# A graph network on one core: the GINE pass takes its neighbour sums from the count matrix, and the attention pass sums the edge attributes

## What is computed

```python
# attention: softmax over the edges of a target (and a self loop), 4 heads
alpha = exp(leaky_relu(a_src[src] + a_dst[dst]) - amax[dst]); alpha /= segment_sum(alpha, dst)[dst]
x = layernorm(x + segment_sum(h[src] * alpha, dst).reshape(N, 256) @ Wl + ...)
# deviation of the neighbours
x = layernorm(x + std of x[src] per dst)
# GINE, with 64 attributes per edge
agg = segment_sum(x[src] + (edge_attr @ We_w + We_b), dst)
x = layernorm(x + relu(((1 + eps) * x + agg) @ W1 + b1) @ W2 + b2)
# four SAGE convolutions 64 -> 128 -> 32 -> 128 -> 64
agg = segment_sum(h[src], dst) / max(deg, 1);  h = agg @ Wl.T + bl + h @ Wr.T
x = layernorm(x + h4)
```

## Time and profile before

| | |
|---|---|
| median of 3 runs | 11377.18 us (11374.62 to 11385.63) |
| span of the profiled execution | 11372.6 us |
| busy, share of the span | PE 65%, POOL 50%, DVE 45%, ACT 16% |
| chain that ended last | PE 35%, issue 19%, DVE 15%, POOL 14%, DVE's queue 11%, DMA 5% |
| DMA | 1416 MB, 125 GB/s mean, 540705 of 977746 packets under 512 bytes |

### The profile page before, as it was taken

How to read it: one execution, slowest core, us unless ns; L and a number is a source line. 1 busy time by engine, 2 the same in 40 slices (tenths; PEclk the granted TensorE clock), 3 DMA queues, 4 the chain that set the end, 5 groups by cost and what they waited for, 6 DMA issues and landing times.

```text
span 11372.6 us, 263999 instructions
## 1 busy us (share of the span) xinstructions
PE 7339.2 (65%) x67389; PEld 5512.0 (48%) x67390; DVE 5137.7 (45%) x13935; ACT 1762.8 (16%) x3566; POOL 5690.5 (50%) x5555
## 2 busy tenths in 40 slices
PE   5888877775466666777954444455677455555676
PEld 4766766664122111445533334445666444444666
DVE  4555555555887777444332233333332333322343
ACT  2333333332033454000000000000000000000000
POOL 4777766553000000753037777776553765653654
PEclk7888888887788899788975555666777676667777
DMA  2333322222012233555532222224556576555566
GB/s 60 74 72 75 73 69 66 65 58 58 18 72 90 113 136 148 160 157 170 179 105 51 54 56 56 57 59 126 187 198 213 183 257 235 183 195 211 201 235 208
DMA packets 977746, 1416.36 MB, mean 125 GB/s; under 512 B 540705, under 2 KB 649761, under 8 KB 970914
## 3 DMA queue, kind: packets, MB, share of 16 engines
q1 hardware_dynamic: 689858, 1130.79, 29.0%
q0 software_dynamic: 184832, 224.29, 9.0%
q10 hardware_dynamic: 102752, 58.62, 1.7%
HBM read 1197.73 MB, written 215.36 MB: 124 GB/s over the span
## 4 chain that ended last, share of the span: by engine, by line
PE 35%; issue 19%; DVE 15%; POOL 14%; DVEq 11%; DMA 5%; ACT 1%; SPq 0%; POOLq 0%; ACTq 0%
PE ps_turn L965 15%; POOL ARENA L650 14%; PE ps_out L811 5%; PE ps_turn L921 4%; DMA ARENA<-counts 3%; PE ps_turn L784 2%; PE ps_pair L811 2%; DVE onehots L1760 2%; DVEq L1774 2%; DVE ARENA L1683 2%; DVE ARENA L1681 1%; PE ps_turn L722 1%; PE ps_pair L846 1%; PE ps_pair L993 1%; DVEq L1688 1%
## 5 line engine op out<-in xcount | busy, mean ns | idle before, releaser
L650 POOL DMA_INDIRECT ARENA<-table_sage,idx x1920 | 1911.9, 996 | 1578.9 <-DVE idx L1755 1041.3
L965 PE MATMUL ps_turn<-ARENA 128*128 128x96 bf16 (+2 forms) x24010 | 2273.8, 260 | 474.5 <-DMA ARENA<-counts 193.2
L965 PEld LDWEIGHTS ps_turn<-ARENA 128*128 128x128 bf16 x24010 | 1847.1, 105 | 896.2 <-issue 589.9
L650 POOL DMA_INDIRECT ARENA<-table_gat,idx x1568 | 1733.1, 1105 | 857.0 <-issue 454.8
L650 POOL DMA_INDIRECT ARENA<-table_gine,idx x1568 | 1541.5, 983 | 964.9 <-issue 953.0
L921 PE MATMUL ps_turn<-ARENA 128*128 128x392 bf16 (+1 forms) x4204 | 1067.6, 360 | 668.0 <-DVE ARENA L1683 458.3
L650 POOL DMA_INDIRECT ARENA<-table_dev,idx x480 | 485.2, 1011 | 1735.5 <-DVE idx L1755 1599.5
L993 PE MATMUL ps_pair<-ARENA,onehots 128*128 128x32 bf16 (+2 forms) x10140 | 685.4, 224 | 931.2 <-DVE ARENA L1767 799.8
L1681 DVE TENSOR_SCALAR ARENA<-ARENA 128x784 bf16<-128x784 f16 (+1 forms) x2102 | 1007.1, 479 | 361.0 <-issue 229.0
L811 PE MATMUL ps_out<-ARENA,onehots 128*128 128x256 f32 (+1 forms) x3136 | 843.8, 432 | 505.5 <-DMA ARENA<-table_gine,idx 351.3
L993 PEld LDWEIGHTS ps_pair<-ARENA,onehots 128*128 x10140 | 562.3, 115 | 1059.7 <-issue 1058.4
(11 more groups left out here) (297 smaller groups left out, 7394.1 us busy)
## 6 DMA issues: line engine op xcount, KB each, us to landing
ARENA<-counts SPq DMA_DIRECT2D x1470, 448.0 KB
counts<-ARENA SPq DMA_DIRECT2D x49, 3136.0 KB, 9.0
ARENA<-counts SPq DMA_DIRECT2D x490, 224.0 KB
ARENA<-dst_b SPq DMA_DIRECT2D x393, 256.0 KB
ARENA<-edge_attr SPq DMA_DIRECT2D x390, 128.0 KB, 2.5
ARENA<-table_sage,idx POOLq DMA_INDIRECT x1920
ARENA<-table_gat,idx POOLq DMA_INDIRECT x1568
ARENA<-table_gine,idx POOLq DMA_INDIRECT x1568
```

Source lines behind the costliest of these rows:

```text
L650: pool.indirect_dma_start(ps["buf"][:, s, c, 0:ps["row"]], None, ps["table"][:, :], bass.IndirectOffsetOnAxis(idx[:, s, c:c + 1], 0)).then ...
L965: last = pe.matmul(ps_dense[half][:, 0:n], RING[:, b, :], XP[:, b, :], start=(b == PIECE_AT[pieces[0]]), stop=(j == pieces[-1] and b == PI ...
```

## The change

The gine pass becomes a dense pass with 64 columns in three parts (`parts=3, row=3 * D`). So dev's node step now stores its rows in three bf16 parts, as the passes before the SAGE passes do. The edge attributes are summed in gat: they are loaded into 64 further columns of the message buffer, the message matmul is 320 columns wide, and `GATW` becomes 325. The sums go to DRAM after each block (`edge_sums`) and come back as `ESUM` for gine's node step. The wider accumulator takes the place of `X` in gat: each block's old rows are loaded from the input again (`old_x`), new rows stand in the accumulator until the pass is over, and three copies then move them to `X`. SRAM areas move accordingly (`WHOLE`, `gat_area`). Edge attributes are padded on the host.

```diff
-GATW = H * D + H + 1
+MSGW = H * D + D
+GATW = MSGW + H + 1
...
-            dict(name="gine", parts=1, n=2 * D, row=D),
+            dict(name="gine", parts=3, n=D, row=3 * D),
...
-        STORING = ["gat", "gine", "sage1", "sage2", "sage3"]
+        STORING = ["gat", "dev", "gine", "sage1", "sage2", "sage3"]
...
-        X = sb("X", [P, TILES, D])
-        ARENA = sb("ARENA", [P, 33602])
+        WHOLE = sb("ARENA", [P, TILES * D + 33602])
+        X = WHOLE[:, 33602:33602 + TILES * D].rearrange("p (t d) -> p t d", d=D)
+        ARENA = WHOLE[:, 0:33602]
...
+        ACC_AT = TILES * D + 33602 - TILES * GATW
+        ACC = WHOLE[:, ACC_AT:ACC_AT + TILES * GATW]
...
-                if passes[k - 1]["parts"] == 1:
-                    with sp.Fori(0, BLOCKS) as b:
-                        load_nodes(b, b)
+                if passes[k - 1]["name"] == "dev":
+                    with sp.Fori(0, STEPS) as b:
+                        load_nodes(b, b + STEPS)
+                    with sp.Fori(0, STEPS) as b:
+                        load_nodes(b + STEPS, b)
+                    sp.wait_ge(rows_ready[k], BLOCKS)
+                    sp.dma_start(ESUM.rearrange("p t d -> p (t d)"), edge_sums).then_inc(edge_sums_loaded, 16)
...
-                            last = pe.matmul(sums[:, 0:H * D if gat else n], lhs, rhs, start=(c == 0 and q == 0), stop=(c == C - 1 and q == parts - 1))
+                            last = pe.matmul(sums[:, 0:MSGW if gat else n], lhs, rhs, start=(c == 0 and q == 0), stop=(c == C - 1 and q == parts - 1))
...
                             pe.wait_ge(ps["first_hot"], g + 2)
+                            pe.wait_ge(edges_loaded[s], i * 16 + 16)
...
                     act.activation(wparts[:, s % 2, :, 0, 0:H], lg[:, 2, :, :], ACT.Exp).then_inc(weight_ready, 1)
 
                     g = i * SLOTS + s
+                    act.dma_start(msg[:, s % 2, :, H * D:MSGW], edge_attr[bass.ds(g * GE, GE), :].rearrange("(p c) d -> p c d", c=C)).then_inc(edges_loaded[s], 16)
...
+                if name == "gat":
+                    act.dma_start(edge_sums[:, bass.ds(blk * (TB * D), TB * D)].rearrange("p (t d) -> p t d", t=TB),
+                                  acc_of[0][:, bass.ds(blk * TB, TB), H * D:MSGW]).then_inc(edge_sums_stored, 16)
...
                 act.wait_ge(step_sem["turned"], block_count("turned", "gat", b))
+                act.wait_ge(product_read, b + 1)
+                settle(act)
+                act.dma_start(old_x, x.rearrange("(t p) d -> p t d", p=P)[:, bass.ds(b * TB, TB), :]).then_inc(old_x_loaded, 16)
...
             if name == "gat":
+                xb = a[:, :, 0:D]
                 ve.wait_ge(step_sem["product"], block_count("product", ps["name"], b))
-                step(ve.tensor_tensor(y, view(ps_gat, D), xb, ALU.add))
+                ve.wait_ge(old_x_loaded, b * 16 + 16)
+                step(ve.tensor_tensor(y, view(ps_gat, D), old_x, ALU.add))
...
                 layer_norm(b, y, xb)
-                ve.sem_inc(rows_ready[k + 1], 1)
+                step(same(view(big, D), xb))
+                store_parts(D)
             if name == "gine":
...
-                step(same(stack[:, :, D:2 * D], a[:, :, D:2 * D]))
+                step(same(stack[:, :, D:2 * D], blocked(ESUM)))
...
+                    step(ve.memset(acc[:, :, H * D:MSGW], 0.0))
...
             def build_vector():
 
+                ve.wait_ge(edge_sums_stored, 16 * BLOCKS)
+                for behind, upto in ((4, 0), (24, 4), (TILES, 24)):
+                    step(ve.tensor_copy(X[:, TILES - behind:TILES - upto, :], acc_of[0][:, TILES - behind:TILES - upto, 0:D]))
                 ve.sem_inc(arena_open, 1)
...
                 step(ve.memset(acc, 0.0))
+                if name == "gine":
+                    step(ve.tensor_scalar(epsb[:, :], epsb[:, :], 1.0, None, ALU.add))
+                    ve.wait_ge(edge_sums_loaded, 16)
```

More of the change, by code:

```diff
@@ L257, in build @@
         for k, ps in enumerate(passes):
-            wide = {"gine": 2 * D}.get(ps["name"], ps["row"])
-            n_buf = SLOTS * C * wide // (1 if ps["parts"] == 1 else 2)
+            n_buf = SLOTS * C * ps["row"] // (1 if ps["parts"] == 1 else 2)
             at = RING_AT + 3136 if ps["name"] == "dev" else SLOTS_AT
@@ L498, in load_idx @@
                 def load_idx(s, g):
-                    sp.wait_ge(ps["slots_free"], g + (order * GROUPS + 1))
+                    sp.wait_ge(ps["slots_free"], g + 1)
                     sp.dma_start(idx[:, s % SLOTS, :], src_r[:, bass.ds(g * C, C)]).then_inc(idx_loaded[s % SLOTS], 16)
[L503 to L511, removed]
@@ new lines, in feed @@
+                for s in range(AHEAD):
+                    load_idx(s, s)
+                with sp.Fori(0, ROUNDS - 1) as i:
+                    for s in range(SLOTS):
+                        load_idx(s + AHEAD, i * SLOTS + (s + AHEAD))
+                        load_dst(s + 1, i * SLOTS + (s + 1))
+                for s in range(SLOTS):
+                    if s + AHEAD < SLOTS:
+                        load_idx(s + AHEAD, (ROUNDS - 1) * SLOTS + s + AHEAD)
+                    load_dst(s + 1, (ROUNDS - 1) * SLOTS + s + 1)
@@ L799, in aggregate @@
                             for q in range(3):
-                                pe.matmul(sums[:, H * D:H * D + (H if q else H + 1)], upper[:, c * P:(c + 1) * P],
+                                pe.matmul(sums[:, MSGW:MSGW + (H if q else H + 1)], upper[:, c * P:(c + 1) * P],
                                           upper_halves(wparts[:, s % 2, c, q, 0:H if q else H + 1]),
@@ L1294, in gat_normalise @@
             dd = small[:, 6, 0:TB * H].rearrange("p (t h) -> p t h", t=TB)
-            step(ve.tensor_scalar(dd, a[:, :, H * D:H * D + H], 1e-16, None, ALU.add))
+            step(ve.tensor_scalar(dd, a[:, :, MSGW:MSGW + H], 1e-16, None, ALU.add))
             step(ve.reciprocal(dd, dd))
@@ L1310, in _ @@
             step(ve.memset(BD[:, :, :], 0.0))
-            step(ve.memset(wparts[:, :, :, :, H:H + 1], 1.0))
             step(ve.memset(DST[:, 0:C], -1.0))
@@ L1481, in _ @@
             ve.sem_inc(dstb_free, 2)
-            node_steps = {"gat": 7, "dev": 19, "gine": 17, "sage1": 6, "sage2": 5, "sage3": 6, "sage4": 11}
+            node_steps = {"gat": 7, "dev": 22, "gine": 17, "sage1": 6, "sage2": 5, "sage3": 6, "sage4": 11}
             def pass_vector(k):
@@ L1594, in pass_vector @@
                     ve.sem_inc(ps["first_hot"], 1)
-                if name == "gine":
-                    step(ve.tensor_scalar(epsb[:, :], epsb[:, :], 1.0, None, ALU.add))
                 ve.sem_inc(ps["first_acc"], 1)
```

76 lines of the change are left out of this document (36 added, 40 removed).

## The result

The change took the time from 11378.18 us (median of 4 runs, 11374.62 to 11385.63) to **10595.66 us** (median of 4, 10585.83 to 10611.35): a ratio of 0.9311, 95% interval 0.93 to 0.9323. The forecast was 10584, the measured time is 12 us above it and inside the range. The profiled execution spans 10591.6 us.

A forecast was written before the change was run, and what follows sets the result against it. POOL's gathers were taken to bound gine and the attention pass up to 1000 us, PE the attention pass after. The terms −1021 + 203 + 25 = −793 us, from 11377.2, gave 10584 us, range 10500 to 10690.

The forecast's parts named there:

- Gine -1021: Gine stage: 2065 us of gathering removed, 1044 put in (start 12 + 3, loops 949, node steps 75, end 5).
- Dev +25: Dev's node step: three more DVE operations before the next sum, 14 × 1.75 us, range 0 to +40.
- Attention pass +203: Attention pass: columns 149, edge rows 15, wider add 7, block ends 18, start memset 5, pass end 9 us.
- Columns, 149: Attention pass from 1000 us: message matmul from 256 to 320 columns, 25% of L811's 595 us on the chain.
- The cover before 1000 us: Attention pass up to 1000 us: POOL hides the wider matmul, cost nothing; 67 us without that cover.
- Edge rows, 15: Attention pass: edge loads cost 15 us, for rounds that find PE idle; range 0 to 163.
- the landing of 2.5 us: Attention pass: edge load assumed to land in 2.5 us, like the old load on SP's queue, leaving 2 us of cover.
- my upper bound of 0.67 us: Attention pass: PE's wait per round if it always waits for edge rows, 0.57 + 2.5 − 2.4; 163 us over 243 rounds.
- The rival that every round pays it: Attention pass: PE waits 0.67 us for edge rows every round after 1000 us, +148, giving 10732 to 10760; chance 0.19.
- Block ends, 18: Attention pass, 14 block ends: ACT's two more DMA issues lengthen PE's idle time, +18 us in all, range 0 to 40.
- The rival that POOL covers all columns: Attention pass: gather-bound beyond the first 1000 us, so the 149 us fall away, giving 10435; chance 0.14.
- the two slow ones: Edge-row wait grown until it sets the round, 11965, chance 0.02; pass stays on gathers, 11605, chance 0.01.

The follow-up runs named there:

- the last run: Kernel before, its gine pass still gathering but without edge loads and with message matmuls of 64 columns in place of 128: 11368.1 us, ratio 0.9992.
- the two kernels without rows: Changed kernel with edge rows neither loaded nor waited for, message matmul 256 columns wide (10441.8 us) or still 320 (10532.4 us).
- the late kernel: Changed kernel with ACT issuing each group's edge load behind that group's one-hot, some 2 us later: 10731.1 us.

## Why the prediction was right, term by term

- **Gine -1021.** Right in its mechanism (POOL set the old pass: by the last run neither the edge loads nor the wider matmul did, and POOL's gathers with their gaps fill it) and in its size: from the end of dev's rows to sage1's first count matmul 2065 us went to 1056.7 (6053.35 to 7110.05), -1008. Start 12.3 us (12), PE's wait ahead of the second unit 5.3, while the edge sums held DVE (3), a step 9 to 11 (10.7), the end 7.6 more than sage1's (5); some 7 us are in no term of mine.
- **Dev +25.** The wait at its step end is 1.95 longer by the rows, 1.75 forecast; the stage with its last parts grew by 22.
- **Attention pass +203.** Measured 199 + 6. That it fits is luck: two terms were wrong by some 55 and 46 us in opposite directions, and the rest came to 46 where 30 were forecast. *Columns, 149:* the step that failed is "25% of the line's share of the chain". The matmuls did get longer about as forecast (eight of them in 2.23 us at the fast level, 1315.81 to 1318.04, where they took 1.82), but a chain's share holds the rest of the round fixed, while the granted clock rose from 0.84 to 0.86 and PE's waits shrank. The price was 91 to 95. The cover before 1000 us held for the most part: by the 141st Exp 14 us of the 91 were spent (traces of the two kernels without rows: 964.3 and 978.3).
- *Edge rows, 15:* the step that failed is the landing of 2.5 us, taken from SP's loads in gine, and with it the few rounds that find PE idle. In the attention pass the load came a median of 3.2 us after its issue (PE went on after 3.4 in the round shown), and PE waited in 87 rounds by the view, in 102 by the semaphore, where 15 us meant some 22. That one wait, 0.65, is near my upper bound of 0.67 is luck: the bound adds the issue's 0.57 to a landing that already counts from the start of the issue, and without it the rows give 0.1. The rival that every round pays it, 10732 or more, is refuted by the time, and most rounds don't wait; that the late kernel comes out at 10731 is chance too, since there 152 rounds wait 1.2 us each.
- *Block ends, 18:* PE's idle time there grew by 23, near the size, and ACT's two issues are 15 of it by the trace in which they stand behind the copy.
- The rival that POOL covers all columns falls with the 91 us; the two slow ones by the time itself.

## What to carry to other kernels

Before making the operation that sets a stage cheaper, see what has to move for it, and price that where it lands: here 1568 gathers were worth 1000 us, and their edge attributes cost 155 elsewhere. A line's share of the chain times its growth was an upper bound here and not the price, since the clock depended on how busy the engine was. And a load used in the round that issues it is worth issuing one wait earlier: that alone took the changed kernel from 10595.7 to 10545.4, the best of these versions together with the one that also reorders the block end (10539.7).

## What the runs showed of the hardware that I had not expected

- Fillers in PE's idle time were nearly free here: 173 us more of them, by width, went with 87 us less of message matmuls and 10 us of time; 221 us fewer lost 24.
- The same 128 KB load landed a median of 2.5 us after its issue beside gine's gathers, and of 3.2 in the attention pass (issue to the last update of its semaphore in the changed kernel's trace). In the late kernel it took 2.6 in the same pass, so the pass alone doesn't set it. The Trainium skill (DMA: Bandwidth & Descriptors, Latency and other measured facts) has a DMA's fixed cost grow with the load on HBM; no run here varied that by itself.
- With eight more matmuls in each of the 488 aggregates of PE's loop, 454 instruction packets of 16 KB were loaded in the attention pass, where the changed kernel has 8, and 22 gaps of about 3 us on PE came with them at the start of the loop's iterations.
